# Second FFN's short tile: gates and ups in one product set, and that tile fourth of six

## What is computed

```python
gate = ghost_linear(x, gate_idx, lut)      # 256 -> 688
up = ghost_linear(x, up_idx, lut)          # 256 -> 688
h = silu(gate) * up
y = ghost_linear(h, down_idx, lut)         # 688 -> 256
x = x + layernorm(y)
```

## Time and profile before

| | us |
|---|---|
| median of 3 runs | 925.39 (925.31 to 927.53) |
| profiled execution, its own time | 927.37 |
| span of that execution | 925.6 |
| TensorE matmul busy | 838.9 (91%) |
| VectorE busy | 767.4 (83%) |
| ScalarE busy | 584.0 (63%) |
| GpSimd busy | 413.6 (45%) |
| mean granted TensorE clock | 0.989 of full |

### The profile page before, as it was taken

One profiled execution on the slowest core, in us unless ns is written; L12 is line 12 of the kernel. 1 busy time (PEld: TensorE's weight loads), 2 busy tenths in 40 slices (PEclk: granted clock), 3 DMA queues, 4 the chain that ended last, 5 costly groups with the idle time before them and its releaser, 6 DMA issues.

```text
span 925.6 us, 12929 instructions
## 1 busy us (share of the span) xinstructions
PE 838.9 (91%) x4314; PEld 580.2 (63%) x4314; DVE 767.4 (83%) x1573; ACT 584.0 (63%) x978; POOL 413.6 (45%) x423
## 2 busy tenths in 40 slices
PE   4889989999999999999999998679787999998997
PEld 2666766776676666666667665457554555554686
DVE  3789999899989999999999998585599687876637
ACT  4668657766778567667667667364545767657531
POOL 2114335344445257777777771171323434443301
PEclk9999999999999999999999999899989999999999
DMA  3497858766877677867867777130000000000001
GB/s 111 76 191 148 156 109 180 159 131 120 200 147 140 134 136 140 153 128 145 168 108 139 134 135 143 33 106 1 1 1 0 1 1 1 2 1 1 1 1 46
DMA packets 276867, 86.29 MB, mean 93 GB/s; under 512 B 267584, under 2 KB 272448, under 8 KB 276416
## 3 DMA queue, kind: packets, MB, share of 16 engines
q1 hardware_dynamic: 275520, 80.05, 44.6%
q0 software_dynamic: 992, 5.34, 2.0%
q10 hardware_dynamic: 288, 0.07, 0.0%
HBM read 17.29 MB, written 1.05 MB: 20 GB/s over the span
## 4 chain that ended last, share of the span: by engine, by line
PE 50%; DVE 29%; issue 8%; ACT 8%; DMA 3%; POOL 1%; SPq 0%; POOLq 0%; DVEq 0%; ACTq 0%
PE ps L1061 11%; PE ps L1062 10%; PE ps L1063 10%; DVE nmax L1683 6%; DVE EP L1698 5%; PE ps L1084 4%; PE ps L1314 3%; PE ps L1099 3%; PE ps L1300 3%; DVE ps L1868 3%; PE ps L1279 2%; DVE ptm L1782 2%; DVE st L1602 1%; ACT EP L1464 1%; DMA ET<-EP 1%
## 5 line engine op out<-in xcount | busy, mean ns | idle before, releaser
L1464 ACT ACTIVATE EP<-ps,rinv 128x1024 f16<-128x1024 f32 x128 | 142.7, 1115 | 53.0 <-DVE rinv L1693 52.1
L1698 DVE SCALAR_TENSOR_TENSOR EP<-ps,rinv,EP 128x1024 f16<-128x1024 f32 x128 | 163.6, 1279 | 5.5 <-ACT EP L1464 4.9
L1454 ACT ACTIVATE ps<-ps,nmax 128x1024 f32<-128x1024 f32 x128 | 139.5, 1090 | 32.2 <-DVE nmax L1683 31.2
L1683 DVE TENSOR_REDUCE nmax<-ps 128x1 f32<-128x1024 f32 x128 | 154.9, 1210 | 2.0 <-PE ps L1063 1.8
L2009 POOL TENSOR_TENSOR wgu<-wgu,ptm 128x688 f32<-128x688 f32 x60 | 100.6, 1677 | 42.9 <-DVE ptm L1782 40.2
L1061 PE MATMUL ps<-ET,VH 128*128 128x512 f16 x256 | 98.2, 384 | 20.8 <-DMA ET<-EP 14.2
L1061 PE MATMUL ps<-KH,QH 128*128 128x512 f32 x256 | 107.2, 419 | 8.8 <-DVE KL L1665 5.1
L2009 POOL TENSOR_TENSOR wdn<-wdn,ptm 128x512 f32<-128x512 f32 x45 | 58.5, 1301 | 95.9 <-DVE ptm L1782 94.4
L1063 PE MATMUL ps<-KH,QL 128*128 128x512 f32 x256 | 100.8, 394 | 0.0
L1062 PE MATMUL ps<-KL,QH 128*128 128x512 f32 x256 | 100.7, 393 | 0.0
L1063 PE MATMUL ps<-ET,VL 128*128 128x512 f16 x256 | 97.8, 382 | 0.0
(11 more groups left out here) (239 smaller groups left out, 2153.1 us busy)
## 6 DMA issues: line engine op xcount, KB each, us to landing
wqr<-in_wqk SPq DMA_DIRECT2D x16, 256.0 KB, 3.6
wgu<-in_tern POOLq DMA_DIRECT2D x3, 1024.0 KB, 6.2
wvr<-in_wv SPq DMA_DIRECT2D x8, 256.0 KB, 4.3
wor<-in_wo SPq DMA_DIRECT2D x16, 128.0 KB, 3.1
ET<-EP SPq DMA_TRANSPOSE x128, 4.4
X<-in_x SPq DMA_DIRECT2D x2, 512.0 KB, 6.0
prw<-in_down_idx POOLq DMA_DIRECT2D x2, 256.0 KB, 6.1
tern<-in_l_wuq_rep SPq DMA_DIRECT2D x1, 512.0 KB, 4.9
```

Of the source, the lines that this page charges most:

```text
L1454: e.activation(bank, bank, ACT.Exp, bias=nmax[:, c:c + 1], scale=1.0, accum_out=rsum[:, c:c + 1]).then_inc(exped.sem, 1)
L1464: e.mul(EP[:, n % NE_RING, 0, :], SB(u, j), rinv[:, c:c + 1]).then_inc(e_hi.sem, 1)
L1683: e.tensor_reduce(nmax[:, c:c + 1], SB(u, j), AX.X, ALU.max, negate=True).then_inc(maxed.sem, 1)
L1698: e.scalar_tensor_tensor(out=EP[:, n % NE_RING, 1, :], in0=SB(u, j), scalar=rinv[:, c:c + 1], in1=EP[:, n % NE_RING, 0, :], op0=ALU.mult, ...
```

## The change

Tile 5 (`PAIRED`) gets one set of six up products. Its 48 gate columns stand at 640 to 687 of the weights of m = 0 and 1 as before, and its 48 up columns are put at 704 to 751 (`UPS`) of the same blocks, so that one product has the gates on partitions 0 to 47 and the ups on 64 to 111 of one bank. `hidden` gates 48 partitions from there. `split_gu` gets a copy and a subtraction of 48 columns for m = 0 and 1, and loses both clearings for m = 2 and 3. The short tile is done fourth of six: after tile 2 and ahead of tile 3, in both halves and in the down products; the first half's turn stands ahead of tile 4. The rows 48 to 127 of the short tile's gating buffer now keep what the tile before left there; the down weights in these rows are all equal.

```diff
+PAIRED, NLAST, UPS = 5, NI - 5 * 128, 5 * 128 + 64
...
-            ("stats", 3, 1, 6, 2), ("hidden", 2, 0), ("hidden", 3, 0)] + norms("norm_in", 3, 4, 4)
-    todo += [("hidden", 4, 0), ("turn_in", 3, 1), ("hidden", 5, 0), ("split",), ("hidden", 0, 1), ("hidden", 1, 1),
-             ("down", 1, 0), ("down", 1, 1), ("hidden", 2, 1), ("stats", 4, 0, 0, 4), ("hidden", 3, 1),
-             ("hidden", 4, 1)] + norms("norm_out", 4, 0, 4)
-    todo += [("hidden", 5, 1), ("split",), ("down", 1, 2), ("stats", 4, 0, 4, 2)] + norms("norm_out", 4, 4, 2)
+            ("stats", 3, 1, 6, 2), ("hidden", 2, 0), ("hidden", 5, 0), ("hidden", 3, 0)] + norms("norm_in", 3, 4, 4)
+    todo += [("turn_in", 3, 1), ("hidden", 4, 0), ("split",), ("hidden", 0, 1), ("hidden", 1, 1),
+             ("down", 1, 0), ("down", 1, 1), ("hidden", 2, 1), ("stats", 4, 0, 0, 4), ("hidden", 5, 1),
+             ("hidden", 3, 1)] + norms("norm_out", 4, 0, 4)
+    todo += [("hidden", 4, 1), ("split",), ("down", 1, 2), ("stats", 4, 0, 4, 2)] + norms("norm_out", 4, 4, 2)
...
-            for o in range(2):
+            for o in range(1 if f == 1 and e == PAIRED else 2):
...
-                    for n in range(NTILE[f]):
+                    for n in TILES[f]:
...
+                if f == 1 and n == PAIRED:
+                    e.scalar_tensor_tensor(out=HF[f][0:NLAST, r, :], in0=ps[64:64 + NLAST, 2 * r, :],
+                                           scalar=SCALES[f][1], in1=SI[f][0:NLAST, r, :], op0=ALU.mult,
+                                           op1=ALU.mult).then_inc(h_mul.sem, 1)
+                    return
+                w.wait_ge(*uped[f, n, half, 1])
...
-                    e.memset(f32(GU[m][:, NI:NIP]), 0.0).then_inc(gu_zero_v.sem, 1)
+                    if m < 2:
+                        e.memset(f32(GU[m][:, NI:NIP]), 0.0).then_inc(gu_zero_v.sem, 1)
+                        w.wait_ge(*gu_zero_v[m])
+                        e.tensor_copy(GU[m][:, UPS:UPS + NLAST], wgu[:, 2 + m, P * PAIRED:NI]).then_inc(gu_hi.sem, 1)
+                        w.wait_ge(*gu_zero_g[m])
+                        w.wait_ge(*gu_hi[m, "up"])
                     w.wait_ge(*gu_hi[m])
-                    w.wait_ge(*gu_zero_v[m])
-                    w.wait_ge(*gu_zero_g[m])
                     e.tensor_tensor(GL[m][:, 0:NI], wgu[:, m, :], f32(GU[m][:, 0:NI]),
                                     ALU.subtract).then_inc(gu_lo.sem, 1)
+                    if m < 2:
+                        w.wait_ge(*gu_lo[m, "gate"])
+                        e.tensor_tensor(GL[m][:, UPS:UPS + NLAST], wgu[:, 2 + m, P * PAIRED:NI],
+                                        f32(GU[m][:, UPS:UPS + NLAST]), ALU.subtract).then_inc(gu_lo.sem, 1)
...
+                    if m >= 2:
+                        continue
```

More of the change, by code:

```diff
@@ L471, in build @@
         SCALES = [(tsc[:, 0:1], tsc[:, 1:2], tsc[:, 2:3]), (1.0, 1.0, 1.0)]
-        NTILE = [8, 6]
+        TILES = [range(8), (0, 1, 2, PAIRED, 3, 4)]
         GU = [QW[0], QW[1], KW[0], KW[1]]
@@ L785, in mark_ffn @@
                 uped.mark(*at, 0)
-                uped.mark(*at, 1)
+                if at[:2] != (1, PAIRED):
+                    uped.mark(*at, 1)
             elif what == "hidden":
@@ L953, in build @@
                 gu_hi.mark(*at)
-                gu_zero_v.mark(*at)
-                gu_zero_g.mark(*at)
+                if at[0] < 2:
+                    gu_zero_v.mark(*at)
+                    gu_hi.mark(*at, "up")
+                    gu_zero_g.mark(*at)
+                    gu_lo.mark(*at, "gate")
                 gu_lo.mark(*at)
@@ L1099, in down @@
                             mm = e.matmul(dst, l, m, start=n == 0 and q == 0,
-                                          stop=n == NTILE[f] - 1 and q == len(pairs) - 1)
+                                          stop=n == TILES[f][-1] and q == len(pairs) - 1)
                     mm.then_inc(downed.sem, 1)
@@ L1634, in hidden @@
                 r = BANK["up_gate", f, n, half][0]
-                w.wait_ge(*uped[f, n, half, 1])
                 w.wait_ge(*gate_on[f, n, half])
```

## The result

The changed kernel takes 934.09 us (931.28 to 936.44, 6 runs) and the kernel before, beside it, 926.31 (925.31 to 927.53, 6 runs): ratio 1.0076, interval 1.0054 to 1.0097. It is slower by 0.8% (5 to 9 us), outside the stated range, on the slower side, which from 928.2 us on had a chance of 0.34. A second measurement gave 931.94 against 926.91, ratio 1.0054 (1.0033 to 1.0074).

What follows compares the result with a forecast made beforehand. It took ScalarE's norms and VectorE's backlog, not TensorE's matmuls, to bound the second FFN's two waits. 0.25 + 1.21 + 0 + 1.0 = 2.46 us on the 925.39 median gave 927.9 us, range 925.6 to 929.6.

Steps and rivals of the forecast that it cites:

- The norms by ScalarE's queue: First half of the second FFN: the second half's norms start 1.21 us later behind ScalarE's queue, all passed on.
- The 48-column subtraction ahead of the shift: Weight splits, m = 0: an extra VectorE subtraction makes TensorE's next matmul 0.25 us later; bounds 0.15 and 0.43.
- For m 2 and 3 a clearing goes on VectorE and on GpSimd, with their waits ... no one waits for these subtractions: Weight splits, m = 2 and 3: clearings and waits removed, subtractions not needed until 865 us, so worth 0.
- The clock behind the turn: After the first half's idle of 3.1 us, TensorE's clock likely falls to half, costing 1.0 us; bounds 0 and 1.5.
- The clock in the tail: Rival, chance 0.22: TensorE's idle of 2.4 us before the last downs causes another clock fall, 1.3 us more.
- The tail: Second half: VectorE's backlog turns the 1.40 us saved on TensorE into idle; worth 0, bounds 0 and -0.1.
- The sum: Whole kernel: 0.25 + 1.21 + 0 + 1.0 = +2.46 us, added to the median of the kernel before.
- The two queue terms: Weight splits and first half: subtraction 0.25 us and late norms 1.21 us, together 1.46 us.
- Two falls: Rival, chance 0.22: the clock falls behind the turn and again in the tail, giving 929.2 us.
- The base of the sum: Whole kernel: the median of the kernel before, 925.39 us, to which all predicted differences were added.

Runs made afterwards that it cites:

- the order alone: The kernel before with only the changed tile orders, keeping two product sets per tile and the old weight splits: 928.60 us, ratio 1.0016.
- the norms-first kernel: The changed kernel with the four norms of the second half's rows put ahead of tile 3's activation: 930.83 us, ratio 1.0032.
- the fillers: The changed kernel with 20 unread matmuls on TensorE in its two idle places, 11 ahead of the turn and 9 in the last-but-one down: 929.44 us, ratio 1.0025.

## Why the prediction was wrong, step by step

- **The norms by ScalarE's queue, 1.21 us.** Right. It is 1.31, and 1.19 for the order alone; the norms-first kernel removes all of it. The small rest stands in VectorE's step into the gating of 48 partitions (below).
- **The 48-column subtraction ahead of the shift, 0.25 us.** It took 0.21 us, as the two sizes gave; the stretch grew by 0.14 to 0.21. That this term and the one above add up to what was measured is partly luck: one was 0.1 too large, the other 0.1 too small.
- **"For m 2 and 3 a clearing goes on VectorE and on GpSimd, with their waits ... no one waits for these subtractions", 0.** This step failed first, a term put at 0. No one waits for the subtractions, but the removed wait had kept VectorE still while GpSimd made masks that TensorE does need. It was priced as a gain that nobody collects, where the question should have been what VectorE runs beside once it is let go. The stretch grew by 1.06 to 1.08 us and the next by 0.1 to 0.4: 0.7 by the waits (put back in the changed kernel, or met in advance in the kernel before, 0.70 and 0.73), 0.36 by what pairing adds, which is only argued to be the 48-column operations.
- **The clock behind the turn, 1.0 us, bounds 0 and 1.5.** Right in kind, a little small. The stretch from the norms to the first down grew by 1.34 and 1.56 us in the two traces of the changed kernel, and the fillers take all of it away. The fall covered the last transposes too, which the term had left out. The bound of 1.5 was one fall of 3.4 us; in the trace with the waits for the clearings back it lasted 6.8 us, like the longer one of the earlier trace rows, and cost 2.41 (13.52 instead of 11.11).
- **The clock in the tail, a rival with 0.22.** Mis-sized as a chance. The gap is 2.16 us, less than the 2.4 us that had held in the earlier trace rows, and yet the clock fell in both traces of the changed kernel and in two more of its versions, and held in one: 1.4 to 1.5 us each time, against the 1.3 given, which had counted only the 2.8 us that these matmuls take at full clock and not the 3.4 us of the fall.
- **The tail, bounds 0 and -0.1.** The two queues were read rightly: 1.40 us of products won, nothing reached the end, and moving VectorE's adds frees 1.58. But 0.35 us were lost. The short gating was taken as equal to a full one, and its own duration is (0.69 us), but 0.25 are the longer steps around the gating of 48 partitions (1.68, 0.62 and 0.71 us instead of 1.57, 0.59 and 0.60); with the second set put back they stay, with the order alone they go, so they are the pairing's. Why this gating does so was not tried. The other 0.10 stands ahead of tile 2's gating, a full tile: 0.53 instead of 0.43 us from the start of the last product, in all nine traces with the edited `hidden` and in none of the four others. The edit also moved that gating's wait for its products behind its other waits; this is the likely cause, but was not tried by itself.
- **The sum.** The two queue terms were 1.46 us, and 1.45 was measured (0.14 + 1.31). The first fall gave 1.34, the masks 1.06 + 0.13, the tail 0.35 and the second fall 1.53: together 5.86, the 5.85 of the table within rounding. "Two falls" would have been the nearest case, and no case had the masks. The remaining 0.86 of this pair of traces lie ahead of the change.
- **The median.** The first three runs of before (925.31 to 927.53) made the kernel look steady; 83 later ones lie between 923.49 and 932.42, with a median of 926.95. The base of the sum, 925.39, was thus 0.9 us under the median beside the changed kernel (926.31) and 1.6 under that of the many. A range of 4 us around one number was narrow for that alone.

## What to carry to other kernels

A matmul in front of a wait is not a cost, and taking it away can be one: count the idle time that it leaves, and look whether the clock survives it. Before an instruction is moved ahead in one engine's list, read what stands behind it in the queues of the others; here 1.3 us of norms were pushed back by one activation and one cast that nobody needed yet. And a wait that goes away starts its engine sooner: see beside whose work it then runs, the masks of GpSimd in this case.

## What the runs showed of the hardware that was not expected

- TensorE's clock fell to its 1.2 GHz level behind waits of 3.07 us (four traces of four), 2.29 (one of one), 2.16 (three of four), and also of 1.67 and 1.55 us; behind 1.74 it held. Behind the last three stand the same single transposes, 0.49 us apart. In the trace of before 2.4 us had held and 2.5 had not the earlier trace rows. How long TensorE waits does not by itself say whether the clock falls; the two falls of the changed kernel's trace lasted 3.4 us each, one in another trace 6.8.
- Eight masks of 128 columns on GpSimd took 4.08 us beside an idle VectorE for most of it, 4.20 with the waits put back and 5.21 beside its copies and subtractions of 688 columns. A single one took 0.29 us with VectorE idle, 0.78 and 1.03 beside a subtraction.
- Twenty matmuls that no one reads made the second FFN, from tile 0's activation on, 2.8 to 3.1 us shorter (53.19 us instead of 56.02 and 56.26).
